# Unread matmuls of constants in the tails of the sparse stages and in the third attention's first slots

## What is computed

```
for L in 0..3:
    x = x + 0.5 * ffn_L(layernorm(x))
    x = x + attn_L(layernorm(x))
    x = x + 0.5 * ffn_L(layernorm(x))
```

```
probs = softmax(x @ W_router);  top_v, top_i = top_k(probs, 2)
y = sum over the two experts e of  probs[e] * down_e(act(up_e(x)))
out = shared(x) + y
```

## Time and profile before

| | |
|---|---|
| median of 3 runs | 3417.91 us (3407.55 to 3426.61) |
| profiled execution | 3410.35 us, span 3408.5 us |
| instructions | 59487 |
| TensorE busy | 2928.4 us, 86% |
| VectorE busy | 2177.0 us, 64% |
| GpSimd busy | 1583.2 us, 46% |
| ScalarE busy | 1431.4 us, 42% |
| mean granted clock | 0.924 |

### The profile page before, as it was taken

How to read it: one execution, slowest core, us unless ns; L and a number is a source line. 1 busy time by engine, 2 the same in 40 slices (tenths; PEclk the granted TensorE clock), 3 DMA queues, 4 the chain that set the end, 5 groups by cost and what they waited for, 6 DMA issues and landing times. The chain is left out here.

```text
span 3408.5 us, 59487 instructions
## 1 busy us (share of the span) xinstructions
PE 2928.4 (86%) x20634; PEld 2564.9 (75%) x20634; DVE 2177.0 (64%) x5538; ACT 1431.4 (42%) x3043; POOL 1583.2 (46%) x1530
## 2 busy tenths in 40 slices
PE   8979999999999899795698977649997858976798
PEld 6859989998898788694487866647775746966687
DVE  6756666666666667665735656548886655665755
ACT  3344555555455433343523333335554334433342
POOL 2333444434444414634605435548887456450743
PEclk9989999999999999897798987959998878988899
DMA  2022212121211200332102333510002352330333
GB/s 70 1 72 55 61 53 68 52 62 52 62 55 49 74 27 1 97 121 63 36 2 80 94 108 90 145 44 2 2 2 69 88 141 81 113 109 3 93 99 97
DMA packets 129129, 220.88 MB, mean 65 GB/s; under 512 B 18609, under 2 KB 68145, under 8 KB 128881
## 3 DMA queue, kind: packets, MB, share of 16 engines
q1 hardware_dynamic: 95026, 147.47, 14.5%
q0 software_dynamic: 21216, 57.96, 6.6%
q10 hardware_dynamic: 12672, 12.58, 1.1%
HBM read 170.23 MB, written 47.72 MB: 64 GB/s over the span
## 5 line engine op out<-in xcount | busy, mean ns | idle before, releaser
L1632 POOL DMA_INDIRECT MXG<-dxn,IDX x250 | 237.3, 949 | 231.6 <-PE bank L1204 167.6
L1642 POOL DMA_INDIRECT YG<-dyo,POSI x192 | 187.4, 976 | 210.6 <-DMA dyo<-YS 111.9
L2491 POOL TENSOR_SCALAR SX<-SX,MN 128x256 f32<-128x256 f32 x256 | 233.7, 928 | 56.4 <-DVE MN L2415 56.3
L1615 POOL TENSOR_TENSOR MWL<-RAW,MWH 128x608 fp32r<-128x608 f32 (+2 forms) x118 | 181.6, 1547 | 42.5 <-ACT MWH L1307 36.2
L1971 POOL TENSOR_TENSOR QL<-QG,QH 128x512 fp32r<-128x512 f32 x64 | 82.9, 1296 | 248.7 <-ACT QH L1826 248.7
L2415 DVE CUSTOM_DVE_ANT_0 SX<-bank,FMASK 128x128 f32<-128x128 f32 (+1 forms) x512 | 156.1, 351 | 50.7 <-PE bank L2305 50.5
L515 PE MATMUL bank<-MWH,GH 128*128 x500 | 172.3, 345 | 8.3 <-issue 4.5
L1026 POOL TENSOR_TENSOR HL<-HID,HH 128x512 fp32r<-128x512 f32 x56 | 72.4, 1293 | 224.2 <-ACT HH L993 223.7
L515 PE MATMUL bank<-MWH,SHH 128*128 128x256 f32 x352 | 111.5, 317 | 73.6 <-POOL SHL L1486 25.4
L1940 POOL TENSOR_TENSOR HWL<-RAW,HWH 128x640 fp32r<-128x640 f32 x68 | 113.3, 1676 | 120.3 <-DVE DEC L1857 120.0
L1329 ACT ACTIVATE GH<-bank 128x256 fp32r<-128x256 f32 x250 | 96.7, 387 | 171.7 <-PE bank L1204 166.0
(11 more groups left out here) (451 smaller groups left out, 11263.0 us busy)
## 6 DMA issues: line engine op xcount, KB each, us to landing
dyo<-YS SPq DMA_DIRECT2D x250, 128.0 KB
RAW<-in_wheads SPq DMA_DIRECT2D x68, 320.0 KB
RAW<-in_eL SPq DMA_DIRECT2D x64, 304.0 KB
BB<-dgates SPq DMA_DIRECT2D x68, 256.0 KB, 3.6
GB<-dgates SPq DMA_DIRECT2D x68, 256.0 KB, 4.3
dxn<-XN ACTq DMA_DIRECT2D x16, 512.0 KB
RAW<-in_eL SPq DMA_DIRECT2D x32, 256.0 KB
RAW<-in_sL SPq DMA_DIRECT2D x18, 384.0 KB
```

Source lines behind the costliest of these rows:

```text
L1615: nc.gpsimd.tensor_tensor(MWL[:, at_:at_ + cols], RAW[:, n % RAW_SLOTS, 0:cols], f32(MWH[:, at_:at_ + cols]), ALU.subtract).then_inc(w_rea ...
L1632: nc.gpsimd.indirect_dma_start(MXG[:, n % XGS, :], None, dxn, bass.IndirectOffsetOnAxis(ap=IDX[:, b:b + 1], axis=0)).then_inc(x_in[n % XGS ...
L1642: nc.gpsimd.indirect_dma_start(YG[:, i % YGS, :], None, dyo[0:m.blocks * P, :], bass.IndirectOffsetOnAxis(ap=POSI[:, c * NT + t:c * NT + t ...
L2491: nc.gpsimd.tensor_scalar(part, part, MN[:, n % RING2, 1:2], None, ALU.subtract).then_inc(s_less1, 1)
```

## The change

In the tail of a sparse stage that has a next stage, once the shared part is over (k above `late`), TensorE waits for x_done of each tile of the slot and then runs ten constant matmuls, into bank 5 if the next stage is sparse and bank 2 if it is an attention. They stand at the end of the slot in TensorE's queue. In L1's tails these are tiles 8 to 15 (slots 7 to 10, 80 matmuls each), in L2's tails tiles 2 to 15 (slots 3 to 9, 140 matmuls each). In the third attention the order of the three opening waits is changed, with 20 constant matmuls between the second and the third, and each of the six slots below 0 begins with six more. That makes 496 new matmuls, with as many weight loads. No result is read from them.

```diff
@@ moe_tensor
                 if 1 <= k <= m.late:
                     shared_down(pe, st, m.early + k - 1)
+                for t in range(NT if nx and k > m.late else 0):
+                    if k == m.slot_of(t):
+                        pe.wait_ge(b_kept, st.blocks + m.blocks)
+                        pe.wait_ge(x_done, st.xd + t + 1)
+                        warm(10, 5 if nx.kind == 'moe' else 2)
@@ attn2_tensor
-            pe.wait_ge(xt_lo, (st.tr + 1) * HALF)
             pe.wait_ge(w_ready, st.pieces + 4)
             pe.wait_ge(prepared, 14)
+            warm(20, 2)
+            pe.wait_ge(xt_lo, (st.tr + 1) * HALF)
             for s in SLOTS2:
+                if s < 0:
+                    warm(6, 2)
                 if 0 <= s < QUADS:
                     scores(s)
```

## The result

The changed kernel took 3454.57 us (median of 4 runs, 3453.20 to 3460.33), the kernel before 3416.56 us beside it (4 runs, 3407.55 to 3426.61). The ratio is 1.0113, 95% interval 1.0094 to 1.0131: the change costs 38 us, 1.1%. I had forecast +7 us, 3425 us, in a range that ended at 3448. The profiled execution spans 3452.2 us, against 3408.5.

The account below looks back on a forecast made before the run. TensorE was busy for 86% of the span, no engine full throughout. Tails +3, +4, +2, +1, third attention -2, start of the stage after tail 2 -1: +7 us on the median 3417.91, so 3425 us, range 3400 to 3448.

Parts of the forecast that it names:

- The order: Tails: 20 constants waiting for x_done stand ahead of the next slot's turn, delaying it; VectorE's low-part waits grow to about 4 us.
- The next 20 run at full clock: Tail 2, slot 9: after a first batch at 4.0 us, the next 20 constants run from 2037.9 to 2040.1.
- tail 1: End of the first L1 stage, into attn1: forecast +3 us.
- tail 2: End of the second L1 stage, into L2: forecast +4 us.
- rival A: Tails and attention: clock falls back between batches, each 20 cost 4.3 us; together +41, 3459 us; chance 0.13.
- Group 0 is hidden behind ScalarE's hold: Tail 1: group 0's turn is late but hidden, as ScalarE is held for 6.9 us.
- tail 3: End of the first L2 stage, into attn2: forecast +2 us.
- tail 4: End of the second L2 stage, into L3: forecast +1 us.
- The last turn, logits and sums at full clock: End of tail 2: they take about half of 2.0 + 1.7 + 1.9 us, some 2.5 us of it on the path.
- The third attention: Its first slots: 3.9 + 0.65 - 4.6 - 1.5 = -1.6 us, taken as -2.
- B: Tails and attention: late turns end in holds or gather waits, the attention wins fully; -3, 3415 us; chance 0.20.
- C: Tails: the holds, 26 us, go as moved slots may miss most; 20 us off the forecast, 3405; chance 0.12.

Follow-up runs that it names:

- e3: Kernel before plus only the two waits for combined tiles in the tails, no constants, attention as before: ratio 1.0012.
- e4: Kernel before plus the tails' 440 constants without the wait for the combined tiles, attention as before: ratio 0.9983.
- e10: Same kernel as e3 (waits alone in the tails) in another set: ratio 1.0032 against the kernel before.
- e11: Same kernel as e4 (tails' constants without the wait) in another set: ratio 1.0024 against the kernel before.
- e15: The change's tails with 16 more constants per slot right behind the group's work, ahead of the waits, attention as before: ratio 1.0116 against the kernel before.
- e5: The changed kernel itself, run again: ratio 1.0122 against the kernel before.
- e14: e13 plus 16 constants without any wait before each tail's last group: 3407.15 us against 3409.72 for the kernel before, ratio 0.9989.
- e2: Kernel before plus only the third attention's constants, tails as before: 3352.13 us, ratio 0.9998.
- e13: Kernel before plus only the third attention's constants, with the 20 ahead of all three waits: ratio 0.9997.
- e1: Kernel before plus only the change's waits and ten constants per combined tile in the four tails: 3372.79 us, ratio 1.0051.
- e7: The change's tails with 30 more constants per slot right behind the group's work, ahead of the waits, attention as before: ratio 1.0245 against the kernel before.
- e9: Kernel before plus tails' constants without the wait and the third attention's constants, its 20 ahead of all three waits: ratio 1.0025.
- e12: The changed kernel itself, run again in another set: ratio 1.0115 against the kernel before.
- e6: The change's tails with three constants per combined tile instead of ten, same waits, attention as before: ratio 1.0071 against the kernel before.

## Why the prediction was wrong

**The order (right).** Turns start behind the batch, behind x_done; VectorE's waits before the low part grow from 1.28 and 2.17 us to 4.24 and 5.25, where I had said about 4. Matmuls behind the wait are the cost, and e3, e4, e10 and e11 show it.

**"The next 20 run at full clock" (wrong; the term that failed).** I priced one batch per tail at 4.0 us and the later ones at 2.2, since at the kernel's start constants between transposes held the clock. There no idle stretch of some microseconds lies between; in the tails one of 3 to 11 us does, in which VectorE combines. In tail 1 the four batches take 4.09, 4.23, 4.42 and 3.97 us, in tail 2 4.23, 4.43, 2.34 and 3.89. Each slot from turn to turn is then about 2 us longer than I had it: the third step of tail 1 is +3.7 us in the first set, +1.8 in e15 where the batch takes 2.34, and I had +1.2. In the four tails 15 batches find the clock low, where I had priced four so. As an estimate, 11 batches of some 1.8 us more each make up to 20 us, of the 27 us by which I missed the tails' sum; how much of it is on the path no total shows. That is rival A's mechanism, and its tails (+7, +14, +4, +9) are close to those measured (+8.6, +13.8, +5.2, +9.2). That its 3459 us are close is in part chance: it had +7 us for the third attention, where 0.7 to 3.3 were measured, and in the first set the same slow batches cost 20 us. I gave it 0.13 and made a mean clock under 0.65 its sign. The mean was 0.66 to 0.78: it averages over batches that begin low and end at full, and says nothing of which matmuls paid. A is wrong in one point: turns right behind a batch do run at full clock, 1.03 to 1.09 us in most slots.

**"Group 0 is hidden behind ScalarE's hold" (half right).** In tail 1 it was: the first low part comes 1.9 us later against the tail's start (+14.7 against +12.8). In tail 2 it comes 5.4 us later, in tail 3 10.6, in tail 4 10.3, since a hold stands behind the late turn or in it, and only in tails 3 and 4 a later one is shorter for that. In the first set, without holds, the first group is late by 2.4 to 3.0 us in all four tails. For tail 2, which had no such hold in my rows, the sum began with group 1 and put group 0 at nothing without a reason. I had treated a hold as an interval of time that swallows what falls into it. It moved with the work.

**"The last turn, logits and sums at full clock" (wrong).** In tails 1 and 2 the last turn takes 2.10 us, in tail 2 its logits and sums (L1117, 1.89 us) are slow as well; of 2.5 us returned nothing was. In tail 3, where the last turn was fast (two halves of 0.66 us), the last step is 8.2 instead of 8.9 us, while in tail 2 of e5, where it was fast as well, the last step is 12.1 us as with the slow one. e4 and e14 say the same: the clock in a tail is worth 0 to 1 us.

**The third attention (nothing, where I had -2).** e2's ratio is 0.9998. The 26 constants took 4.62 us, as 3.9 and 0.65 of the sum. The returns up to the first scores were right: e13, where the 20 hide, has its first mask 3.4 to 4.3 us earlier, against 4.6 less 0.65. The 1.5 us behind the first scores did not come: there the clock is down again (0.57 in the changed kernel from 2300 to 2316 us). Without them the sum is 0, and 0.7 was measured in the first profile, 2.3 to 3.3 in the two later ones.

**The rivals.** B (everything swallowed) is out: e1 costs 20 us with hardly a hold. C named the right suspect on one side: the holds are not fixed. They did not go: they came at other places, and to TensorE too. The Trainium skill, "Runtime: NRT & Kernel Launch", section "Instruction fetch mechanics", has blocks of 16 KiB; from it I had estimated four more blocks for TensorE and no new hold. The queue view has the four, and its packets are of some 16.4 kB (2.26 MB in 138). Before and after read:

```profile
q8 instruction: 134, 2.20, 0.3%
q14 instruction: 81, 0.66, 0.1%
```

```profile
q8 instruction: 138, 2.26, 0.3%
q14 instruction: 81, 0.66, 0.1%
```

(packets, MB, share of 16 engines). q8 follows TensorE's constants over all kernels: 134 with none in the tails, 135 with three per tile, 137 or 138 with ten, 142 and 146 with 16 and 30 more. That no hold is new was wrong: constants or transposes that wait for nothing and come some 1 to 2 us apart appear early in tails 3 and 4 with ten or more constants per tile (the changed kernel, e5, e7, e9, e11, e12, e15; in e7, e9 and e11 in tails 1 and 2 too), not with three (e6) or the waits alone (e10), and all of it in the sets where the kernel before takes over 3400 us.

**Open.** What the holds are. That TensorE's come with more instructions, and that the queue of instruction packets grows, is an association; the packets themselves take about 1 us each, and I found none at the place of several holds. Why one set had almost none and was some 60 us faster is not known; the record gives the same chip number for it as for the third set, and doesn't say whether it is the same chip. How the cost divides between the clock and the holds in the other sets. And what e6 costs outside the tails.

## What to carry to other kernels

Matmuls that only warm TensorE must not stand between a wait on the ring and the instruction that the ring needs: put them ahead of the wait, in the idle time itself, and not behind it. By the medians 440 of them without the wait cost between -4 and +8 us; with it they cost 20 us in the first set, and with the attention's 56 beside them 38 to 42 us in the first measurement and in two later sets. Price each batch by the idle stretch ahead of it and not by what the batch before did; the mean granted clock of a stretch does not tell which instructions were slow. And first ask whether anyone waits for the engine's speed: here the clock of a tail went from 0.50 to 0.80, and the tail stayed as it was.

## What the runs showed of the hardware

- Transposes do run at full clock behind constants, 1.03 to 1.09 us for eight against 2.10. The Trainium skill, "TensorE: Matmul & The Clock Gate", section "Part 4: PE-mode transpose", says that the full clock does not engage for them; where a batch stood right ahead, these runs don't agree. Whether transposes alone would raise the clock no run here tested.
- A batch of 20 behind 0.2 to 1.9 us of idleness took 2.34 us in most places (e1, e5, e7, e15), though 4.04 to 4.43 where the constants just before had run at the low clock or been held (e7, e11, e12); behind 2.7 to 3.3 us between 2.34 and 4.43; behind 3.4 to 11 us 3.7 to 4.4.
- The same program took 3352 us in one set and 3410 to 3419 in three others, four tails with the instructions of the kernel before 148 (e2) and 170 to 173 us. The share of a cost that a trace shows as holds can be absent in the next set.
- In the stretches in which TensorE was held while it waited for nothing, it still ran one matmul every 0.7 to 2.8 us (e7, e11, the changed kernel).
